# Two transformer layers on one core: value weighings with 64 stationary columns instead of 128, and two small loads moved into the first layer

## The reference

```python
x = L0_attn_x
xn = _layernorm(x, axis=-1)
x = x + _L0_attn_ref(xn, ...) + _L0_ffn_ref(xn, L0_ffn_W1, L0_ffn_W2, L0_ffn_W3)
xn = _layernorm(x, axis=-1)
x = x + _L1_attn_ref(xn, ...) + _L1_ffn_ref(xn, L1_ffn_w_gate, L1_ffn_w_up, L1_ffn_w_down)

def _L1_attn_ref(x, W_qkv, b_qkv, W_out, b_out):      # h, e = 16, 32
    q, k, v = jnp.split(x @ W_qkv.T + b_qkv, 3, axis=-1)
    scores = jnp.einsum('bqhe,bkhe->bhqk', q, k) * scale
    scores = jnp.where(causal[None, None], scores, -jnp.inf)
    attn = jax.nn.softmax(scores, axis=-1)
    out = jnp.einsum('bhqk,bkhe->bqhe', attn, v)
    return out.reshape(b, l, d) @ W_out.T + b_out
```

## Time and profile before

| what | value |
|---|---|
| median of 3 runs | 1747.48 us (1744.93 to 1747.74) |
| the profiled execution | 1748.79 us, its span 1747.0 us |
| mean granted TensorE clock | 0.989 of full speed |
| busy: PE, PEld, DVE, ACT, POOL | 97%, 78%, 60%, 42%, 16% of the span |
| first layer | 0 to about 641 us |
| projection | 642 to about 771 us |
| attention | 772 to about 1169 us |
| end of the second layer | 1171 to 1747 us |

### The profile page before, as it was taken

How to read it: one execution, slowest core, us unless ns; L and a number is a source line. 1 busy time by engine, 2 the same in 40 slices (tenths; PEclk the granted TensorE clock), 3 DMA queues, 4 the chain that set the end, 5 groups by cost and what they waited for, 6 DMA issues and landing times. The chain is left out here.

```text
span 1747.0 us, 22877 instructions
## 1 busy us (share of the span) xinstructions
PE 1690.6 (97%) x8318; PEld 1365.9 (78%) x8318; DVE 1044.7 (60%) x1795; ACT 733.9 (42%) x1528; POOL 286.8 (16%) x280
## 2 busy tenths in 40 slices
PE   5999999999999989989999999989999999999998
PEld 3677888788788878867777777768888888888887
DVE  4321365564623454459999999964655654655776
ACT  4521322232213332249999999972222222222221
POOL 3201210310310112100000000013154031033220
PEclk9899999999999999989999999999999999999999
DMA  7200110110101038833445445514010010012243
GB/s 280 102 17 1 61 49 19 55 31 25 55 7 37 30 113 269 298 147 95 122 136 139 127 123 142 139 48 151 1 48 25 1 48 25 0 49 65 81 133 132
DMA packets 75663, 149.59 MB, mean 86 GB/s; under 512 B 9497, under 2 KB 26521, under 8 KB 74018
## 3 DMA queue, kind: packets, MB, share of 16 engines
q1 hardware_dynamic: 75554, 148.17, 27.0%
HBM read 101.87 MB, written 46.27 MB: 85 GB/s over the span
## 5 line engine op out<-in xcount | busy, mean ns | idle before, releaser
L1560 DVE TENSOR_TENSOR pt_lo<-p_turn,pt_hi 128x512 fp32r<-128x512 f32 (+3 forms) x384 | 200.8, 550 | 18.4 <-ACT pt_hi L1533 14.3
L1553 DVE TENSOR_REDUCE row_top<-p_score 128x1 f32<-128x128 f32 (+7 forms) x256 | 189.5, 750 | 15.5 <-PE p_score L1485 15.3
L1525 ACT ACTIVATE prob<-p_score,row_top 128x128 f32<-128x128 f32 (+7 forms) x256 | 190.0, 745 | 6.3 <-DVE row_top L1553 5.5
L1533 ACT ACTIVATE pt_hi<-p_turn 128x512 fp32r<-128x512 f32 (+3 forms) x384 | 182.5, 494 | 5.5 <-PE p_turn L1496 1.6
L1496 PE MATMUL p_turn<-ident,prob 128*128 128x128 f32 x1152 | 181.5, 276 | 1.3 <-DVE pt_lo L1560 1.0
L1019 DVE TENSOR_TENSOR hid<-hid,p_up 128x512 f32<-128x512 f32 x64 | 44.0, 688 | 218.7 <-PE p_up L484 203.0
L1896 DVE TENSOR_TENSOR e_hid<-e_hid,e_p_up 128x512 f32<-128x512 f32 x64 | 44.0, 687 | 196.2 <-PE e_p_up L1782 196.2
L1511 PE MATMUL p_o<-pt_hi,v 128*128 128x512 f32 (+3 forms) x384 | 148.6, 395 | 4.0 <-ACT o_both L1543 3.2
L1496 PEld LDWEIGHTS p_turn<-ident,prob 128*128 128x128 f32 x1152 | 131.8, 141 | 14.9 <-DVE pt_lo L1560 1.7
L1483 PE MATMUL p_score<-stack 128*128 128x512 f32 (+3 forms) x384 | 128.3, 389 | 7.1 <-PEq L54 3.5
L766 ACT ACTIVATE hid<-p_gate 128x512 f32<-128x512 f32 x64 | 38.3, 599 | 217.3 <-PE p_gate L484 217.2
(11 more groups left out here) (272 smaller groups left out, 4027.1 us busy)
## 6 DMA issues: line engine op xcount, KB each, us to landing
stack<-qk_parked SPq DMA_DIRECT2D x256, 128.0 KB, 3.9
raw<-in_wgu SPq DMA_DIRECT2D x64, 256.0 KB, 2.6
qk_parked<-qk SPq DMA_DIRECT2D x16, 1024.0 KB, 4.0
v_parked<-v_out SPq DMA_DIRECT2D x16, 512.0 KB, 5.6
v<-v_parked SPq DMA_DIRECT2D x8, 1024.0 KB, 9.4
o_parked<-o_both SPq DMA_DIRECT2D x64, 128.0 KB
res<-in_x SPq DMA_DIRECT2D x8, 512.0 KB
rot<-in_w2t SPq DMA_DIRECT2D x4, 1024.0 KB, 8.0
```

Source lines behind the costliest of these rows:

```text
L1525: act.activation(row_at(h, r, 0, width_of(r)), p_score[:, r % 2, 0:width_of(r)], ACT.Exp, bias=top[:, r:r + 1], accum_out=sums).then_inc(e ...
L1533: act.activation(pt_hi[:, (BL * h + j) % PT, c0:W], p_turn[:, (BL * h + j) % TB, c0:W], ACT.Copy).then_inc(rounded, 1)
L1553: dve.tensor_reduce(top[:, r:r + 1], p_score[:, r % 2, 0:width_of(r)], AX_X, ALU.max, negate=True).then_inc(topped, 1)
L1560: dve.tensor_tensor(pt_lo[:, slot, c0:W], p_turn[:, (BL * h + j) % TB, c0:W], pt_hi[:, slot, c0:W].bitcast(F32), ALU.subtract).then_inc(sp ...
```

## The change

1. The stationary side of a weighing is the 64 columns of one head. Its output goes to partitions 0 to 63 of `p_o` for every head, and `read_o` always reads these.
2. The loads of bias and scale move from the projection's first two DMAs to SP's queue in the first layer, behind L308. Their tiles and their semaphore are handed over, as those of the weights are.

```diff
--- before.py
+++ after.py
@@ -77,6 +77,9 @@
     rounded: list
     split: list
     done: object
+    bias: object
+    scale: object
+    consts: object
...
@@ -306,6 +309,8 @@
             sp.wait_ge(d_turned, NC * NG)
             for i in range(2):
                 sp.dma_start(ahead.raw[:, i], t["wqk"][0, i]).then_inc(ahead.loaded[i], 16)
+            sp.dma_start(ahead.bias[:], t["qk_bias"]).then_inc(ahead.consts, 16)
+            sp.dma_start(ahead.scale[:, 0:1], t["qk_scale"]).then_inc(ahead.consts, 16)
             for q in range(QUARTERS):
                 store_res(q)
...
@@ -1167,9 +1172,8 @@
         raw_v = sb("raw_v", [P, KD, D])
         v_hi = sb("v_hi", [P, KD, D], F32R)
         v_lo = sb("v_lo", [P, KD, D], F32R)
-        bias = sb("bias", [P, 2 * QUADS])
+        bias, scale, consts = ahead.bias, ahead.scale, ahead.consts
         pair_bias = sb("pair_bias", [P, 2])
-        scale = sb("scale", [P, 1])
         one = sb("one", [P, 1])
...
@@ -1177,7 +1181,7 @@
-        consts, one_set, scale_done = sem("consts"), sem("one_set"), sem("scale_done")
+        one_set, scale_done = sem("one_set"), sem("scale_done")
...
@@ -1205,8 +1209,6 @@
-            sp.dma_start(bias[:], qk_bias).then_inc(consts, 16)
-            sp.dma_start(scale[:], qk_scale).then_inc(consts, 16)
             for k in range(KD):
                 sp.dma_start(raw_v[:, k], wv[:, k]).then_inc(wv_loaded, 16)
             body(0, False)
@@ -1506,10 +1508,10 @@
                 pe.wait_ge(split, BL * (HB * it + h) + j + 1)
-                lhs = v[:, b, kb, 2 * pr:2 * pr + 2].rearrange("p a h e -> p (a h e)")
+                lhs = v[:, b, kb, 2 * pr + a].rearrange("p h e -> p (h e)")
                 slot = (BL * h + j) % PT
-                pe.matmul(p_o[:, c0:W], lhs, pt_hi[:, slot, c0:W], start=(kb == 0), stop=False)
-                pe.matmul(p_o[:, c0:W], lhs, pt_lo[:, slot, c0:W], start=False,
+                pe.matmul(p_o[0:2 * E, c0:W], lhs, pt_hi[:, slot, c0:W], start=(kb == 0), stop=False)
+                pe.matmul(p_o[0:2 * E, c0:W], lhs, pt_lo[:, slot, c0:W], start=False,
                           stop=(j in (QB - 1, BL - 1))).then_inc(weighted, 1)
@@ -1534,13 +1536,12 @@
             def read_o(it, h, g):
-                a = h % 2
                 act.wait_ge(weighted, BL * (HB * it + h) + (BL if g else QB))
...
-                act.activation(o_both[:, (G * h + g) % OS], p_o[64 * a:64 * a + 64, :], ACT.Copy).then_inc(o_read, 1)
+                act.activation(o_both[:, (G * h + g) % OS], p_o[0:2 * E, :], ACT.Copy).then_inc(o_read, 1)
...
@@ -1975,6 +1976,7 @@
         handed = alloc(nc, ctx)[2]
+        qk_bias, qk_scale = sb("qk_bias", [P, HEADS // 2]), sb("qk_scale", [P, 8])
         raw0_at = nc.sbuf_base
...
@@ -1984,7 +1986,7 @@
-                      handed("job_done"))
+                      handed("job_done"), qk_bias, qk_scale, handed("qk_consts"))
```

More of the change, by code:

```diff
@@ L1150, in load_values, with project_qkv @@
     sp.dma_start(v[:, b].rearrange("p t a h e -> p (t a h e)").bitcast(F32), v_dram[B * quad + b]).then_inc(loaded, 16)
-def project_qkv(nc, wqk, wv, qk_bias, qk_scale, masks, x_hi, x_lo, qk_dram, v_dram, stack, v_first, mask, ahead, qk_parts, qk_stored):
+def project_qkv(nc, wqk, wv, masks, x_hi, x_lo, qk_dram, v_dram, stack, v_first, mask, ahead, qk_parts, qk_stored):
     QUADS = HEADS // 4
@@ L2009, in two_layers @@
             mask = sb1("mask", [P, 2, P], BF16)
-            phase(nc, project_qkv, t["wqk"], t["wv"], t["qk_bias"], t["qk_scale"], t["masks"], x_hi, x_lo, qk_dram,
+            phase(nc, project_qkv, t["wqk"], t["wv"], t["masks"], x_hi, x_lo, qk_dram,
                   v_dram, stack, v, mask, ahead, qk_parts, qk_stored)
```

## The result

The changed kernel takes 1758.6 us, median of 4 runs (1755.89 to 1761.51), beside 1746.89 for the kernel before. The ratio is 1.0070, with a 95% interval from 1.0054 to 1.0086: slower by 11.7 us. The forecast was 1740.1, 7.4 us faster. The profiled execution took 1755.89 us (span 1754.1).

A forecast was written before the change was run, and what follows sets the result against it. The attention was taken to be bound by the loop through PE, ACT and DVE, all nearly full. Gains of 5.9 + 0.3 + 0.3 + 0.87 = 7.4 us gave 1740.1 us by the median, range 1737.0 to 1744.6.

The forecast's parts named there:

- Reads at partition 0: Attention: all heads read p_o like even ones, so ACT's long leg shrinks and 0.38 us per head pair goes, 5.9 us.
- Rival (A): Attention: the slow odd-head read does not come from its partition; gain only 2.9 us, 1744.6; chance 0.13.
- The tail: End of the attention: the last head's two reads and last weighings stand in line, so some 0.3 us gained.
- Shorter loads: Attention weighings on PE: loading 64 instead of 128 stationary columns saves 0.056 us where not hidden, 0.3 us in all.
- Rival (C): Attention: PE empties itself between 128 and 64 columns, 0.16 us a change, 16 a head; about 1800 us; chance 0.09.
- Bias and scale earlier: Projection's start: DVE and PE start 2.47 us earlier, but POOL's value weights only 0.87, so 0.87 us gets through.
- Rival (B): Projection: DVE's wait for the mask takes the 0.87 us back; gain 6.5 us, 1741.0; chance 0.12.
- The two loads added to the first layer's end: End of first layer: SP's two added issues delay nothing that anyone waits for, put at 0.

The follow-up runs named there:

- e4: Kernel before, 128-column weighings kept, but both heads of a pair read from partitions 0 to 63 (computes something else): 1739.95 us, ratio 0.9966.
- e2: Kernel before with part one of the change alone (64-column weighings, reads at partition 0), tiles where they were: 1738.61 us, ratio 0.9952.
- e3: Whole change, but bias and scale tiles placed behind the first layer's last tile so no other tile moves, against the kernel before: 1739.31 us, ratio 0.9963.
- e13: e3 plus POOL waiting for each of the four value-weight pieces by itself instead of all four, against the kernel before: 1736.88 us, ratio 0.9944.
- e1: Kernel before with an unused 64-byte tile per partition ahead of everything behind x_lo, no instruction changed: 1767.74 us, ratio 1.0117.
- e12: e2 plus 224 unused bytes ahead of pt_hi, so the attention's moving tiles match v modulo 256, against the kernel before: 1739.71 us, ratio 0.9966.
- e6: Separate measurement, not the kernel: 48 matmuls per pair of tile places, DVE and ACT idle, then at work; 0.2267 to 0.2344 us start to start.
- e9: Separate measurement, not the kernel: finer table of tile distances to 480 bytes, plus narrower forms; 512-column streams on 128 stationary columns 0.2267 to 0.2341 us.

## Why the prediction was wrong, step by step

- Reads at partition 0, 5.9 us: right, 5.79 in e4, with the alternation gone in the place where it was read. Rival (A) is out. The tail, put at 0.3, gave 0.16.
- Shorter loads, 0.3: right in kind, 0.42 (e2 against e4). A load lasts 136 to 139 ns on the weighings' lines, where the line between the earlier trace rows gave 136.
- Rival (C), PE emptying itself between 128 and 64 columns: out. 0.23 us at the change back to 128 columns (890.08 to 890.31 in the changed kernel), as in the earlier trace rows, and the attention got shorter, 389.29 us instead of 395.72. The loss of 0.16 us a change that the rival reckoned with shows in no run.
- Bias and scale earlier, 0.87: wrong in its size, 0.37 in the profiled execution (the value product starts 32.61 us after the first layer's last matmul, before 32.98) and nothing that the medians of e3 (1739.31) and e2 (1738.61) show. The step that failed was that an issue 0.87 us earlier lands 0.87 us earlier. The last pieces landed later instead, and why stays open. Rival (B) named the mask as what takes the gain back; it was not that: the gain was gone ahead of the value product, and in e13, where it wasn't, only 0.23 of 2.58 us are lost behind it. DVE's wait for the mask is 8.8 us, before 8.9.
- The step that turned the sign and made the forecast fail: "The two loads added to the first layer's end ... I put them at 0". The reason given was that SP's issues delay nobody, and no run shows that they do. What costs is that the tiles they fill are allocated ahead of everything else, which the sum had no term for: about +21 us (e1) against -8 (e2). By the medians the two add up to 1759.9 where 1758.6 was measured. No row of the profile of before could have shown it, but two columns of it and the allocation could have raised the question: `p_o<-pt_lo,v`, whose tiles stood apart, had 0.2326 us from start to start, the groups on x 0.227.
- The profiled changed kernel lost only 3.3 us in the first layer, e1 9.7. At the start of the program the clock falls at varying times: between 8 and 128 us it was 0.97 and PE did 459 matmuls in the changed kernel, 0.94 and 436 before, 0.94 and 438 in e1. e12, whose first layer is that of the kernel before in every place and instruction, had 0.97 and 460, so this varies from run to run and is no part of the change. Behind 150 us the changed kernel and e1 lose the same: the 1248 matmuls that stream x there take 296.3 us in either, before 289.8.

## What to carry to other kernels

A new tile is a change to every tile behind it. When a small tile is added, put it behind the others, as e3 does. Rounding its size up to 256 bytes in a partition should do as well: an estimate from e6 and e9 (0.2267 us at a distance of 0, 0.2268 to 0.2274 at 256), not tried in a whole kernel. And compare the mean length of the untouched matmul groups before and after: here a shift of 1.5% in all groups that share one operand (nearly 3% from start to start) was a matter of place. And when an engine is let start earlier, ask what its first handed-over input waits for: here one wait for the last of four pieces swallowed 2.4 us.

## What the runs showed of the hardware that I had not expected

- A 128 x 512 matmul on a 128-column stationary tile cost 0.2267 to 0.2276 us where both tiles started at the same place modulo 256 bytes, 0.229 where the moving one lay 64 further, 0.232 to 0.234 elsewhere (all multiples of 32; e6, e9), with DVE and ACT busy or not for places up to 96 (e6). With 64 stationary columns it was 0.229 to 0.230 at all three distances tried (e9).
- ACT did not overlap the read of `p_o` at partitions 64 to 127, written to partitions 0 to 63, with its neighbours: 0.17 us before it and 0.14 behind it; with every read at partition 0 the attention of 32 heads took 5.96 us less (e4). Whether it is the start at 64 or the move to other partitions was not tried.
- Ahead of the value product, idleness of PE of 2.76 and 3.29 us was followed by 3.4 us at a clock of 0.50, idleness of 1.82 to 2.54 by none (single profiles of five kernels). At the projection's start 2.65 us in the changed kernel were followed by a low stretch as well (645.8 to 649.2, a clock of 0.50).
